# VectorE's instruction loops with several rounds per turn instead of one, in a two-block metaformer kernel

## The reference, cut to what matters

```python
x = x + linear_attention(ln(x))                     # softmax over positions of k and v
t = t + moe(ln(t))                                  # 8 experts, 128 -> 512 -> 128, exact gelu, top 2 of 8
x = x + grouped_conv3x3(ln(x))                      # 8 groups of 16 channels
t = t + ode(ln(t))                                  # below

f = lambda z: tanh(tanh(z @ W1.T + b1) @ W2.T + b2) @ W3.T + b3      # 128 -> 512 -> 512 -> 128
for _ in range(255):                                # one step per position, all 16 images at once
    k1 = f(y); k2 = f(y + dt/2*k1); k3 = f(y + dt/2*k2); k4 = f(y + dt*k3)
    y = y + dt * (k1 + 2*k2 + 2*k3 + k4) / 6
```

## Time and profile before

| | us |
|---|---|
| median of 3 runs (2952.31 to 2953.3) | 2952.32 |
| the profiled execution's own time | 2953.22 |
| its span, first to last instruction | 2951.4 |
| PE busy | 2847.4 (96%) |
| VectorE busy | 2366.2 (80%) |
| ScalarE busy | 1417.0 (48%) |
| granted TensorE clock, mean | 0.98 |

### The profile page before, as it was taken

How to read it: one execution, slowest core, us unless ns; L and a number is a source line. 1 busy time by engine, 2 the same in 40 slices (tenths; PEclk the granted TensorE clock), 3 DMA queues, 4 the chain that set the end, 5 groups by cost and what they waited for, 6 DMA issues and landing times.

```text
span 2951.4 us, 197650 instructions
## 1 busy us (share of the span) xinstructions
PE 2847.4 (96%) x76994; PEld 2331.3 (79%) x76994; DVE 2366.2 (80%) x12835; ACT 1417.0 (48%) x8958; POOL 587.9 (20%) x903
## 2 busy tenths in 40 slices
PE   7789999999999999999999999999999999999999
PEld 3478888888888888888888878888887777777777
DVE  4668888888888888888888878888877777777777
ACT  5455555555555555565554444444433333333333
POOL 5023232332323323233331001111100000000000
PEclk9779999999999999999999999999999999999999
DMA  3000000000000000000000000000000000000000
GB/s 115 0 12 11 11 14 11 14 11 11 14 11 14 11 12 13 11 14 11 14 11 5 0 0 1 0 0 0 8 8 0 0 0 0 0 0 0 0 0 14
DMA packets 21977, 28.15 MB, mean 10 GB/s; under 512 B 4384, under 2 KB 12896, under 8 KB 21544
## 3 DMA queue, kind: packets, MB, share of 16 engines
q1 hardware_dynamic: 21928, 27.48, 3.0%
HBM read 25.24 MB, written 2.23 MB: 9 GB/s over the span
## 4 chain that ended last, share of the span: by engine, by line
PE 88%; DVE 5%; ACT 4%; issue 2%; DMA 0%; SPq 0%; DVEq 0%; ACTq 0%; POOLq 0%; POOL 0%
PE PSUM L616 32%; PE PSUM L622 28%; PE PSUM L677 12%; PE PSUM L607 6%; PE PSUM L684 4%; DVE PSUM L1234 3%; ACT HA L934 2%; PE PSUM L714 1%; PE PSUM L643 1%; PE PSUM L647 1%; PE PSUM L454 1%; PE PSUM L448 0%; PE PSUM L656 0%; PE PSUM L486 0%; PE PSUM L690 0%
## 5 line engine op out<-in xcount | busy, mean ns | idle before, releaser
L1234 DVE TENSOR_REDUCE PSUM<-PSUM 128x32 f32<-128x64 f32 x4080 | 872.4, 232 | 168.5 <-PE PSUM L622 114.7
L616 PEld LDWEIGHTS PSUM<-HA,RL 128*128 128x128 f16 x16320 | 553.5, 96 | 306.2 <-ACT HA L934 297.0
L935 ACT ACTIVATE PSUM<-PSUM 128x32 f32<-128x32 f32 x4080 | 786.4, 194 | 0.0
L934 ACT ACTIVATE HA<-PSUM 128x32 f16<-128x32 f32 x2040 | 404.9, 199 | 722.6 <-DVE PSUM L1234 722.5
L934 ACT ACTIVATE HB<-PSUM 128x32 f16<-128x32 f32 x2040 | 405.1, 200 | 714.6 <-DVE PSUM L1234 714.6
L616 PE MATMUL PSUM<-HA,RL 128*128 128x16 f16 x16320 | 718.1, 170 | 31.2 <-ACT HA L934 7.5
L616 PE MATMUL PSUM<-HB,RLU 128*128 128x16 f16 x16320 | 716.8, 170 | 6.8 <-ACT HB L934 0.2
L622 PE MATMUL PSUM<-HA,RH 128*128 128x32 f16 x16320 | 652.9, 177 | 0.0
L622 PE MATMUL PSUM<-HB,RHU 128*128 128x32 f16 x16320 | 651.8, 177 | 0.0
L616 PEld LDWEIGHTS PSUM<-HB,RLU 128*128 128x128 f16 x16320 | 550.8, 96 | 71.9 <-ACT HB L934 2.4
L622 PEld LDWEIGHTS PSUM<-HA,RH 128*128 128x128 f16 x16320 | 566.0, 96 | 0.0
(11 more groups left out here) (229 smaller groups left out, 3071.5 us busy)
## 6 DMA issues: line engine op xcount, KB each, us to landing
G<-scores SPq DMA_DIRECT2D x64, 256.0 KB, 3.1
N<-in_x SPq DMA_DIRECT2D x8, 256.0 KB, 4.6
NHL<-in_w SPq DMA_DIRECT2D x1, 2048.0 KB, 10.4
STF<-in_w SPq DMA_DIRECT2D x1, 2048.0 KB, 15.1
out<-W2HL SPq DMA_DIRECT2D x8, 256.0 KB, 2.4
G<-in_r SPq DMA_DIRECT2D x1, 1024.0 KB, 5.4
R1K<-in_r SPq DMA_DIRECT2D x1, 256.0 KB, 2.7
R3F<-in_r SPq DMA_DIRECT2D x1, 256.0 KB, 5.6
```

Source lines behind the costliest of these rows:

```text
L616: mm(out[m // 2][:, 2 * B * (m % 2):2 * B * (m % 2) + B], lo[:, k, m], src[:, k, 0], start=False, stop=False)
L934: A(hi[:, 2 * h:2 * h + 2, 0], src, ACT.Tanh, scale=1.0 / scale).then_inc(rk_hi, 1)
L935: A(full, src, ACT.Tanh, scale=1.0 / scale).then_inc(rk_f, 1)
L1234: v.tensor_reduce(bank[:, SUM:SUM + 2 * B].rearrange("p (m b) -> p m b", m=2), bank[:, 0:4 * B].rearrange("p (m c b) -> p m b c", m=2, c=2 ...
```

## The change

Only VectorE's program is changed. `rounds` gets a number `per` and writes `per` rounds into the body of its loop, so the loop turns `(count - 1) // per` times. The loop of plain steps holds 11 steps. All four numbers divide the counts (63 = 9 x 7, 7 = 1 x 7, 15 = 3 x 5, 77 = 7 x 11), so the same rounds and steps are done, in the same order.

```diff
-            def rounds(start, count, beside):
+            def rounds(start, count, per, beside):
                 part(start, beside(0, True), 0, EDGE)
-                with dve.Fori(0, count - 1) as i:
-                    part(start + 2 * i, beside(i, False), EDGE, SLOTS)
-                    part(start + 2 * (i + 1), beside(i + 1, False), 0, EDGE)
+                with dve.Fori(0, (count - 1) // per) as n:
+                    for i in range(per):
+                        i = n * per + i
+                        part(start + 2 * i, beside(i, False), EDGE, SLOTS)
+                        part(start + 2 * (i + 1), beside(i + 1, False), 0, EDGE)
                 part(start + 2 * (count - 1), beside(count - 1, False), EDGE, SLOTS)
...
-            rounds(1, GROUPS, experts_beside)
+            rounds(1, GROUPS, 7, experts_beside)
             moe_tail(step, expert)
-            rounds(S_STAT, NT, lambda t, opening: lambda slot: statistics(t, slot))
-            rounds(S_CONV, B, lambda t, opening: lambda slot: conv(t, slot))
-            with dve.Fori(S_OUT, STEPS) as s:
-                step(s, False)
+            rounds(S_STAT, NT, 7, lambda t, opening: lambda slot: statistics(t, slot))
+            rounds(S_CONV, B, 5, lambda t, opening: lambda slot: conv(t, slot))
+            with dve.Fori(0, (STEPS - S_OUT) // 11) as n:
+                for r in range(11):
+                    step(S_OUT + 11 * n + r, False)
```

## The result

The changed kernel took 3015.68 us (median of 6 runs, 3014.31 to 3016.66) against 2953.30 before (6 runs), a ratio of 1.021 with the 95% interval 1.0199 to 1.0221. It is slower by 62 us, where +19 was forecast and the range ended at 3000. The direction was right, and so was the place of the 16 stops that the forecast assumed. The size was not, and there were stops at a place that the forecast had excluded.

What follows compares the result with a forecast made beforehand. The prediction took the layer ring PE, VectorE, ScalarE, PE as the bound. Removed branches gave -13.1 us and 16 reloads of 2.0 us +32, so +18.9 us on 2953.2, forecast 2972 us, range 2938 to 3000.

Steps and rivals of the forecast that it cites:

- Seams removed: VectorE's taken branches in experts, statistics, convolution and plain steps: 142 go, at 0.08 to 0.11 us each, saving 13.1 us.
- The bodies no longer fit and 16 branches reload: VectorE's unrolled loop bodies exceed its instruction store, so the 16 remaining taken branches wait for code: 32 us added.
- Price of a reload: At each of VectorE's 16 remaining branches, loading the body's first piece again costs 2.0 us, range 0 to 3.1.
- "A reload" as one transfer: At VectorE's 16 remaining branches: one 8 KB piece is fetched per branch, 2.0 us, and later code is loaded ahead.
- stalls anywhere but at the loops' ends: Sign in VectorE's timeline that would make the prediction wrong; it expected stalls only at 16 layers, at the loops' ends.
- The rival of the costly reload: At VectorE's 16 branches a reload costs much more than a plain transfer: 5 us each, +67 us, 3020; chance 0.11.
- Clock holds: Behind the 16 stops the granted clock may hold, since 2 us is shorter than ScalarE's table change; nothing added.
- the second rival: Each stall of VectorE also costs granted clock: some 16 us in all on top of the reloads, 2988; chance 0.17.
- Straight code does not stall: Within VectorE's unrolled bodies, code is loaded ahead, so crossing a piece's edge without a branch costs nothing.
- the fourth rival: Unrolled code stalls at some 140 piece edges on VectorE, 0.1 us each: 14 us more, 2986; chance 0.05.

Runs made afterwards that it cites:

- the straight version: The changed kernel with all four of VectorE's loops written out entirely, no branch in the ODE, waits against constants: 2939.64 us, ratio 0.9949.
- changed, shifted by 10: The changed kernel with 10 one-element memsets at the start of VectorE's program, moving every later instruction by 10 places: 3001.79 us, ratio 1.0162.
- the useless reductions: The straight version with a useless reduction of some 3 us at the 16 places where the changed kernel branches back: 2991.07 us, ratio 1.0124.

## Why the prediction was wrong

Each kernel's layers were set against the straight version's, from all starts of L1234 between the third and the 254th step; the sums in us:

| | seams | first stops | second stops | half clock and edges | sum |
|---|---|---|---|---|---|
| before | 15.8 | - | - | - | 15.8 |
| changed | - | 42.5 (16 x 2.66) | 13.4 (8 x 1.68) | 21.0 | 77.0 |
| changed, shifted by 10 | - | 42.4 | - | 21.4 | 63.8 |

77.0 - 15.8 = 61.2; the profiled executions differ by 3014.31 - 2953.22 = 61.1.

- *Seams removed*: the mechanism and the place were right, the forecast took 13.1 for 142 seams, and against the straight version all 158 cost 15.8, 0.10 each (14.2 for 142; the seams of the 16 turns that are left are inside the stops). The straight version's full gain of 14.6 us (medians) confirms it. Between the stops a plain step of the changed kernel takes 10.70 us (median; 10.71 forecast) and an expert round 21.62, where 21.54 was forecast; the straight version has the 21.54.
- *The bodies no longer fit and 16 branches reload*: right, on less evidence than it had seemed; the limit turned out to be 3 pieces touched, far below the bodies in question.
- *Price of a reload*: the term that was mis-sized first. 2.0 us was taken from data transfers; measured are 2.66 us on the path. The rows give the span from issue to landing, and a reload has more behind it. The data rows end when the bytes have landed, and the load of the piece itself takes 0.3 to 0.6 us; from the branch's end to its start on the queue it is 1.0 us, and from its end to VectorE's next instruction 1.4 (in the first turn: branch until 355.9, load from 356.9 to 357.4, next instruction at 358.9). 16 x 0.66 = 10.6 us.
- *"A reload" as one transfer*: the step that failed. The sum had one piece per branch, and the prediction called stalls anywhere but at the loops' ends a sign that it is wrong. The next piece is asked for only when the head piece is entered, and the expert body's head stood 4 instructions ahead of its end, so 8 branches paid for two loads: 13.4 us. The rival of the costly reload named it ("several pieces must come before VectorE goes on") and rightly said that nothing in the rows spoke for it; but where the edges lie could have been worked out from the program's order and the load times of before. Its 3020 lies near the measured time by luck, since it stood for 16 stops of 5 us, and the dearest turn here paid 4.3 us for its two loads.
- *Clock holds*: wrong, the second rival came true beside the forecast. It gave 16 us; layers that touch half clock hold 12.3 us, besides the stops. A stop of 2 us was thought short enough for the clock to hold. The stops came out longer; PE idled for 2.5 to 2.8 us at each, and the clock fell behind all 16.
- *Straight code does not stall*: wrong by 8.8 us, the fourth rival's mechanism at some 0.06 us per edge instead of 0.1. My argument against it, that the first pass through the new bodies showed nothing, rested on fewer than ten edges.

From the forecast: 18.9 + 10.6 + 13.4 + 12.3 + 8.8 - 2.7 (the seams gave 15.8, not 13.1) = 61.3 us, against 61.2 in the layers. No single term carries the miss: the shifted version, which has no second stops, still took 3001.79 us, beyond the range's end of 3000. Three of the rivals were not alternatives to the forecast but came on top of it. All three have one sign, since each begins with a stop or a load that the forecast itself assumed, and a range made of separate cases missed their sum.

The two terms behind the stops can be told apart in the expert turns by how long the half clock lasted. In the shifted version, with one stop per turn, it lasted 3.4 us behind five of the eight expert stops and 6.8 us behind three, as in these two windows:

```profile
982.00:985.30 3.30, 3.30 (x79) 2.46 (x77) 2.42 (x14) 1.00 (x8) 0.31 (x1) 0.50 0.00 0
...
1135.50:1142.30 6.80, 5.80 (x134) 4.41 (x135) 4.51 (x25) 1.98 (x16) 0.53 (x2) 0.50 0.00 1
```

The layers behind a stop cost 0.7 us in the first case and 1.2 in the second. With the useless reductions it is the same, 0.6 to 0.7 us seven times and 1.2 once. In the changed kernel, where PE idles a second time in the second stop (1.4 to 1.6 us), all eight lasted 6.8 us and cost some 1.15 us. The other 0.6 of its 1.8 us per turn lies in layers at full clock, beside loads. Why the half clock lasts longer behind one single stop than behind another stays open.

## What to carry to other kernels

Before a loop body of a side engine is unrolled, count the 128-instruction pieces that it touches: on VectorE bodies in 3 pieces were not loaded again, and bodies in 4 or more cost 2.7 us per turn, or 4.3 with the head just ahead of an edge, whatever their size, and the clock on top. Unroll to stay within that (2945.94 us here), or write the loop out altogether with constant waits (2939.64); what lies between paid here for the reloads and for the edges. When a forecast assumes stops on the critical chain, add the clock and the next transfer behind each stop to it rather than keep them as alternatives.

## What the runs showed of the hardware that was not expected

- A shift by 25 instructions outside the path moved a kernel by 175 us (3120.98 to 2945.94), and by 10 instructions by 14 us.
- A taken branch on VectorE to code that is present cost 0.08 to 0.11 us of the chain; to code that is absent 2.66, behind bodies of 297 to 4777 instructions alike in the experts, convolution and plain steps.
- PE's granted clock fell to 1.2 GHz behind each stop of some 3 us on VectorE, though PE itself idled for only 2.4 to 2.8 us at a time. It stayed there for 3.4 or 6.8 us, most of them with PE busy.
- Straight code with constant waits crossed pieces almost for nothing (0.6 us for 106 loads), unrolled loops with register waits at some 0.06 us per edge.
